# Latent-attention layer: context products in other slots, probabilities turned straight behind the scores, the first group's rows gathered and mixed by tiles

## The reference, cut to what matters

```
x = x + experts(layernorm(x))                       # end of layer 0: slots_out gathered by slot, weighted by wt
h = layernorm(x)
kv = h @ Wkv_down.T ; q = h @ Wq.T ; k = kv @ Wk_up.T ; v = kv @ Wv_up.T
x = x + (softmax(q k^T / 8) v) @ Wo.T               # latent attention
h = layernorm(x)
q = h @ xWq + bq ; k = ctx @ xWk + bk ; v = ctx @ xWv + bv
x = x + softmax(masked(q k^T / 4)) v @ xWo + bo     # cross-attention
x = x + ffn(layernorm(x))                           # quantised gate, up and down products
```

## Time and profile before

| what | value |
|---|---|
| median of three launches | 1798.15 us (1794.9 to 1802.68) |
| the profiled launch | 1803.34 us, its span from first to last instruction 1801.6 us |
| busy share of the span | PE 87%, DVE 53%, ACT 46%, POOL 26% |
| mean granted TensorE clock | 0.931 |
| layer1's slots (first scores to last scores) | 986.5 to 1414 us of the span |

### The profile page before, as it was taken

The page is one execution under the profiler, slowest core; times in us unless marked ns, Lnnn a source line. Parts: engine busy times, 40 slices in busy tenths (PEclk is TensorE's granted clock), DMA queues, the critical chain, the costliest instruction groups (busy, mean ns, idle before and its releaser), DMA issues. The chain is left out here.

```text
span 1801.6 us, 26868 instructions
## 1 busy us (share of the span) xinstructions
PE 1563.5 (87%) x10059; PEld 1083.7 (60%) x10059; DVE 960.3 (53%) x2226; ACT 828.9 (46%) x1819; POOL 459.5 (26%) x582
## 2 busy tenths in 40 slices
PE   6999999998986569999995999999999869994099
PEld 3666766666664348878783666666667634441088
DVE  3555666756765324222213655656564545499932
ACT  3346564554555212121212556556565523596740
POOL 3123223243334310000005654544433200131000
PEclk9999999998988679999996999999999979996599
DMA  3330111111221153353433111110100000000211
GB/s 107 141 145 20 44 28 40 32 41 40 58 80 39 56 165 123 105 158 106 143 108 106 36 37 31 51 51 13 28 16 16 13 12 0 1 0 1 93 35 59
DMA packets 99681, 107.12 MB, mean 59 GB/s; under 512 B 25315, under 2 KB 88557, under 8 KB 99553
## 3 DMA queue, kind: packets, MB, share of 16 engines
q1 hardware_dynamic: 93408, 88.83, 15.7%
q0 software_dynamic: 6144, 16.57, 2.8%
HBM read 63.59 MB, written 42.01 MB: 59 GB/s over the span
## 5 line engine op out<-in xcount | busy, mean ns | idle before, releaser
L1866 ACT ACTIVATE c_pr<-bank,c_nmax 128x256 f32<-128x256 f32 x256 | 117.9, 475 | 153.7 <-DVE c_nmax L1947 131.8
L1619 POOL TENSOR_SCALAR c_pr<-c_pr,c_rsum 128x256 f32<-128x256 f32 x256 | 127.6, 513 | 228.3 <-DVE c_rsum L1952 228.2
L1336 PE MATMUL bank<-b_XT,shared 128*128 128x320 f32 x512 | 154.6, 437 | 0.0
L1386 ACT ACTIVATE b_G<-bank 128x320 f32<-128x320 f32 x128 | 55.9, 437 | 210.9 <-PE bank L1336 210.9
L1350 PE MATMUL bank<-shared,b_G 128*128 128x256 f32 x640 | 142.2, 379 | 0.0
L1350 PEld LDWEIGHTS bank<-shared,b_G 128*128 128x128 f32 x640 | 120.9, 190 | 17.8
L947 DVE TENSOR_TENSOR a_A<-bank,a_causal 128x512 f32<-128x512 f32 x128 | 79.5, 683 | 77.4 <-PE bank L475 77.4
L1947 DVE TENSOR_REDUCE c_nmax<-bank 128x2 f32<-128x512 f32 x128 | 82.3, 684 | 59.0 <-PE bank L1658 58.2
L1336 PEld LDWEIGHTS bank<-b_XT,shared 128*128 128x128 f32 x512 | 92.5, 193 | 27.6 <-issue 1.2
L412 POOL TENSOR_TENSOR a_L<-a_L,a_Lm 128x1232 f32<-128x1232 f32 x32 | 72.0, 2249 | 141.5 <-DVE a_Lm L962 135.9
L1405 DVE COPY b_Y<-bank 128x256 f32<-128x256 f32 x80 | 34.0, 425 | 120.3 <-PE bank L1350 120.1
(11 more groups left out here) (314 smaller groups left out, 3448.7 us busy)
## 6 DMA issues: line engine op xcount, KB each, us to landing
shared<-L_ffn_w SPq DMA_DIRECT2D x32, 512.0 KB
t_slots_in<-a_h SPq DMA_DIRECT2D x20, 512.0 KB, 6.8
shared<-t_slots_in SPq DMA_DIRECT2D x15, 640.0 KB, 7.0
t_slots_out<-b_Y SPq DMA_DIRECT2D x15, 640.0 KB, 4.1
a_xin<-x SPq DMA_DIRECT2D x8, 512.0 KB, 3.8
a_xr<-x SPq DMA_DIRECT2D x8, 512.0 KB, 3.8
t_x_a<-hT_all SPq DMA_DIRECT2D x8, 512.0 KB, 2.9
shared<-t_x_a SPq DMA_DIRECT2D x8, 512.0 KB
```

What stands on the lines that cost most here:

```text
L1336: t = p.matmul(P[2 + n % 2][:, 0:HC], w1[e % 3][:, u, 128 * f:128 * f + 128], XT[e % 2][:, u, HC * m:HC * m + HC], start=(u == 0), stop=(u ...
L1619: p.tensor_scalar(pr[k][:, e, u, :], pr[k][:, e, u, :], rsum[k][:, e, u:u + 1], 1.0, ALU.mult, ALU.mult).then_inc(q.pr_ready, 1)
L1866: a.activation(pr[t % 2][:, e, u, :], P[e][:, S * u:S * u + S], ACT.Exp, bias=nmax[t % 2][:, e, u:u + 1], accum_out=sums[t % 2][:, e, u:u ...
```

## The change

It does the following, all in layer1:

- turn(t - 1) on PE moves to right behind scores(t), ahead of values(t - 2) and all extra work.
- xk and xv are made in slot 7 of their own group, ahead of project0, and copied out by ACT in slot 0 of the next group, behind heads and ahead of the xturn and q3 copies. (Before: made in slot 1, copied in slot 2.)
- xm is made in slot 1, behind turn_norm 0, and copied in slot 2 (before: 3 and 4). penalties runs in slot 2 behind moments(2) (before: slot 4, ahead of by_key).
- vo is made in slot 2 behind project1, and its addition runs in slot 3, ahead of by_key (before: both in slot 5).
- UNITS follows, so that banks 5 to 7 are handed out in another order. By that order the bank of xturn (or of q3 in group 1) is the one that xk held, the bank of q3 is that of xv, turn0b has xout0's, xm has xout1's, latk has lat's and q0 has turn2a's.
- The first group's gathers are issued tile by tile (both choices of tile 0, then of tile 1, and so on), each tile with a semaphore of its own; mix_first waits for one tile at a time, adds both choices and takes that tile's bn_stats.

```diff
--- before.py
+++ after.py
@@ -1499,13 +1499,14 @@
         xPT = sb("xPT", [S2, T])
         amax = sb("amax", [128, 1])
 
-        q = signals(nc, st, "c_pool c_dve rows0 rows1 stored "
+        q = signals(nc, st, "c_pool c_dve tile0 tile1 tile2 tile3 rows0 rows1 stored "
                             "absorb_psum absorb_kept mixed st0 st1 st2 mo0 mo1 mo2 ve0 ve1 ve2 rs0 rs1 rs2 h0 h1 h2 sh0 sh1 sh2 "
                             "s_psum nmax_ready exp_ready rsum_ready pr_ready pt_psum PTa_ready PTd_ready a_psum aT_ready "
                             "kept_dve L_kept L_ready xmax_ready xe_ready xr_ready  amax_part amax_ready "
                             "made0 made1 made2 kept0 kept1 kept2")
         sq = c.second_signals
         r_in, x_in, rows_in = (sq.slot0_in, sq.slot1_in), (sq.x0_in, sq.x1_in), (q.rows0, q.rows1)
+        tile_in = (q.tile0, q.tile1, q.tile2, q.tile3)
         stat_s, mom_s, var_s, rstd_s, h_s = ((q.st0, q.st1, q.st2), (q.mo0, q.mo1, q.mo2), (q.ve0, q.ve1, q.ve2),
                                              (q.rs0, q.rs1, q.rs2), (q.h0, q.h1, q.h2))
         shift_s = (q.sh0, q.sh1, q.sh2)
@@ -1521,13 +1522,13 @@
 
 
         UNITS = {0: (("xturn", -2, 1), ("q3", 0, 1), ("xout0", -2, 2), ("xout1", -2, 2)),
-                 1: (("turn0a", 1, 1), ("turn0b", 1, 1), ("xk", -1, 2), ("xv", -1, 2)),
-                 2: (("project1", -1, 1),),
-                 3: (("lat", 1, 1), ("xm", -1, 2)),
+                 1: (("turn0a", 1, 1), ("turn0b", 1, 1), ("xm", -1, 2)),
+                 2: (("project1", -1, 1), ("vo", -1, 1)),
+                 3: (("lat", 1, 1),),
                  4: (("turn2a", -2, 1), ("turn2b", -2, 1), ("latk", 1, 1), ("q0", 1, 1)),
-                 5: (("vo", -1, 1), ("q1", 1, 1), ("turn1a", -1, 1), ("turn1b", -1, 1)),
+                 5: (("q1", 1, 1), ("turn1a", -1, 1), ("turn1b", -1, 1)),
                  6: (("q2", 1, 1), ("xs", -1, 1)),
-                 7: (("project0", 0, 1),)}
+                 7: (("xk", 0, 2), ("xv", 0, 2), ("project0", 0, 1))}
         place, used, filled = {}, [0, 0, 0], [0, 0, 0]
         turn_of = 0
         for t in range(FIRST, LAST):
@@ -1596,7 +1597,7 @@
                             p.wait_ge(q.mixed, 2 * NT * (i - 1))
                     p.indirect_dma_start(out=rows[k][:, m // NT, m % NT, :], out_offset=None, in_=dr["slots_out"],
                                          in_offset=bass.IndirectOffsetOnAxis(ap=slot[k][:, m:m + 1], axis=0),
-                                         bounds_check=SLOTS - 1, oob_is_err=False).then_inc(rows_in[k], 16)
+                                         bounds_check=SLOTS - 1, oob_is_err=False).then_inc(rows_in[k] if i else tile_in[m % NT], 16)
 
                 def deviation(n, i):
 
@@ -1620,10 +1621,10 @@
                                                 ALU.mult, ALU.mult).then_inc(q.pr_ready, 1)
                     if s in (6, 7) and there(g + 3):
                         for m in range(2):
-                            gather(g + 3, 2 * (s - 6) + m)
+                            gather(g + 3, 2 * (s - 6) + m if g + 3 else NT * m + s - 6)
                     if s in (0, 1) and there(g + 2):
                         for m in range(2):
-                            gather(g + 2, 4 + 2 * s + m)
+                            gather(g + 2, 4 + 2 * s + m if g + 2 else NT * m + 2 + s)
 
             @block.tensor
             def _(p):
@@ -1789,6 +1790,8 @@
                     late, behind, ahead = there(g - 2), there(g - 1), there(g + 1)
                     if there(g):
                         scores(t)
+                    if 0 <= t - 1 < NG * NS:
+                        turn(t - 1)
                     if 0 <= t - 2 < NG * NS:
                         values(t - 2)
                     if s == 0 and late:
@@ -1805,21 +1808,16 @@
                         turn_norm(2, g - 2)
                     if s == 4 and ahead:
                         latent_keys(g + 1)
-                    if s == 5 and behind:
+                    if s == 2 and behind:
                         x_outputs(g - 1)
                     if s == 5 and ahead:
                         queries(g + 1, 1)
                     if s == 6 and ahead:
                         queries(g + 1, 2)
-                    if 0 <= t - 1 < NG * NS:
-                        turn(t - 1)
                     if s == 0 and late:
                         x_values(g - 2, 0)
                         x_values(g - 2, 1)
                     if s == 1 and behind:
-                        context("xk", g - 1, xwk)
-                        context("xv", g - 1, xwv)
-                    if s == 3 and behind:
                         x_keys(g - 1)
                     if s == 4 and ahead:
                         queries(g + 1, 0)
@@ -1828,6 +1826,8 @@
                     if s == 6 and behind:
                         x_scores(g - 1)
                     if s == 7 and there(g):
+                        context("xk", g, xwk)
+                        context("xv", g, xwv)
                         project(g, 0)
 
             @block.scalar
@@ -1899,6 +1899,9 @@
                         exponents(t)
                     if 0 <= t - 2 < NG * NS:
                         heads(t - 2)
+                    if s == 0 and behind:
+                        keep_context("xk", g - 1, kbT, bk)
+                        keep_context("xv", g - 1, vbT, bv)
                     if s == 0 and late:
                         keep_unit("xturn", g - 2, xPT[:, :], bank("xturn", g - 2)[0:S2, :])
                     if s == 0 and there(g):
@@ -1906,12 +1909,9 @@
                     if s == 1 and ahead:
                         keep_norm(0, g + 1, [hT0[:, u, :] for u in range(2)])
                     if s == 2 and behind:
-                        keep_context("xk", g - 1, kbT, bk)
-                        keep_context("xv", g - 1, vbT, bv)
+                        keep_unit("xm", g - 1, xm[:, :, :, :].rearrange("p c b k -> p (c b k)"), bank("xm", g - 1)[:, 0:2 * KX])
                     if s == 3 and ahead:
                         keep_unit("lat", g + 1, latT[(g + 1) % 2][:, :], bank("lat", g + 1)[:, :])
-                    if s == 4 and behind:
-                        keep_unit("xm", g - 1, xm[:, :, :, :].rearrange("p c b k -> p (c b k)"), bank("xm", g - 1)[:, 0:2 * KX])
                     if s == 4 and late:
                         keep_norm(2, g - 2, [c.hT_all[:, u, T * (g - 2):T * (g - 2) + T] for u in range(2)])
                     if s == 5 and ahead:
@@ -1960,16 +1960,30 @@
                 def mix(i, k):
                     if k == 0:
                         v.wait_ge(x_in[i % 2], 32 * (i // 2 + 1))
-                        v.wait_ge(rows_in[i % 2], 16 * TOPK * NT * (i // 2 + 1))
+                        v.wait_ge(rows_in[i % 2], 16 * TOPK * NT * ((i + 1) // 2))
                     for j in range(NT):
                         if k:
                             v.wait_ge(q.mixed, 2 * NT * i + j + 1)
                         v.scalar_tensor_tensor(x3[i % 3][:, j, :], rows[i % 2][:, k, j, :], wt[i % 2][:, NT * k + j:NT * k + j + 1],
                                                x3[i % 3][:, j, :] if k else xin[i % 2][:, j, :], ALU.mult, ALU.add).then_inc(q.mixed, 1)
 
+                def mix_first():
+
+                    v.wait_ge(x_in[0], 32)
+                    for j in range(NT):
+                        v.wait_ge(tile_in[j], 16 * TOPK)
+                        for k in range(TOPK):
+                            if k:
+                                v.wait_ge(q.mixed, 2 * j + 1)
+                            v.scalar_tensor_tensor(x3[0][:, j, :], rows[0][:, k, j, :], wt[0][:, NT * k + j:NT * k + j + 1],
+                                                   x3[0][:, j, :] if k else xin[0][:, j, :], ALU.mult, ALU.add).then_inc(q.mixed, 1)
+                        v.wait_ge(q.mixed, 2 * j + 2)
+                        v.bn_stats(stats[0][:, j, :], x3[0][:, j, :]).then_inc(stat_s[0], 1)
+
                 def moments(n, i, x):
-                    for j in range(NT):
-                        v.bn_stats(stats[n][:, j, :], x[:, j, :]).then_inc(stat_s[n], 1)
+                    if n or i:
+                        for j in range(NT):
+                            v.bn_stats(stats[n][:, j, :], x[:, j, :]).then_inc(stat_s[n], 1)
                     v.wait_ge(stat_s[n], NT * (i + 1))
                     if i:
                         v.wait_ge(h_s[n], NT * i)
@@ -2060,11 +2074,10 @@
                         shifts(2, g - 2)
                     if s == 4 and behind:
                         shifts(1, g - 1)
-                        penalties(g - 1)
                     if s == 5 and there(g + 1):
                         wait_full(v, "latk", g + 1)
                         v.tensor_copy(lat[(g + 1) % 2][:, :, :].rearrange("p j r -> p (j r)"), bank("latk", g + 1)[:, 0:NT * LR]).then_inc(freed("latk", g + 1), 1)
-                    if s == 5 and behind:
```

(9 more changed lines are left out.)

## The result

The changed kernel takes **1807.31 us** (median of 7; 1805.38 to 1809.35) against 1798.22 before (median of 7): ratio 1.0047, 95% interval 1.0035 to 1.0060. It is 0.5% slower; the forecast was 1797.9, no change. The profiled launch has a span of 1805.6 us.

What follows compares the result with a forecast made beforehand. PE was taken as the bound (busy 402.5 of layer1's 427.9 us), so only its waits could be won. The terms summed to -0.2 us, 1803.1 profiled; 5.2 off for the median gave 1797.9 us, range 1784 to 1809.

Steps and rivals of the forecast that it cites:

- start: Group 0's tile-wise start: POOL's power, queued behind group 1's gathers, moves only to 968.0; -1.6 us, bounds 0 and -3.4.
- groups 0 and 1, with the extra product: Early turns wait for POOL, busy with gathers: +1.5 us; one more context product made by the last scores: +2.2.
- group 7: Last group with scores: slot 0 has the new wait and little is won, +1.6 us, bounds 0 and +3.
- end: Behind the last scores: vo addition ahead of moments(1); last x_scores +1.5 us later counted from last turn, bounds -1 and +3.
- The new slots, groups 2 to 6: Steady groups: waits of 4.1 us a group against 4.6 before, -2.4 us over five groups, bounds -9 and +6.
- A slot's fixed part: PE's scores, values and turn in every slot: 2.08 us for the first two plus 0.87 for the turn, 2.96.
- Slot 0: xturn waits for ACT's copy out of xk's bank: new wait of 1.7 to 1.8 us, every group from 1 to 7.
- rival D: Start of group 0: the tile-wise start brings nothing, POOL being the queue in front; 1799.5 us, chance 0.10.
- Clock: PE's granted clock over layer1: 5 us lost now, 2 afterwards, so -3 us; bounds -5 and +15.
- Rival B: PE's two waits per group each halve the clock behind them, twelve at 1.7 us; 1816.3 us, chance 0.10.
- Rival C: Turns wait for POOL in all short slots, about 0.5 us each, +15 us; 1812.9 us, chance 0.07.
- Rival A: The waits forecast at slots 0 and 4 are short, half of each, with no clock loss; 1786.3 us, chance 0.23.

Runs made afterwards that it cites:

- Experiments 6: The changed kernel with ACT's two context copies moved from slot 0 to the end of slot 7 and the turn behind values(t - 2): 1784.54 us, ratio 0.9924 to before.
- 8: The kernel before with only the turn moved, to right behind values(t - 2) (the turn third): 1782.08 us, ratio 0.9907.
- 11: The changed kernel with only the turn moved, to right behind values(t - 2): 1799.46 us, ratio 1.0011 to the kernel before.
- experiment 4: The changed kernel with ACT's two context copies moved from slot 0 to the end of slot 7: 1793.96 us, ratio 0.9978 to the kernel before.
- experiment 2: The kernel before with only turn(t - 1) moved, to right behind scores(t) (the turn ahead): 1792.41 us, ratio 0.9971.
- experiments 1: The kernel before with only the first group's gathers and mix done by tiles: 1795.61 us, ratio 0.9992.
- 9: The kernel before with the turn right behind values(t - 2) and the tile-wise first group, no moved context work: 1778.52 us, ratio 0.9885.
- experiments 5: The kernel before with the turn right behind scores and the tile-wise first group, no moved context work: 1790.81 us, ratio 0.9952.
- 10: The changed kernel with context copies in slot 7, the turn behind values, and the last group's vo addition behind moments(1): 1785.47 us, ratio 0.9924 to before.
- 7: The changed kernel with the first group gathered and mixed as before, without tiles: 1810.06 us, ratio 1.0059 to the kernel before.

## Why the prediction was wrong, point by point

It lay inside its range, but on the wrong side of no change: -0.2 us in the sum, 9.1 measured. In the profiled pair, term by term:

| term of the sum | forecast | measured |
|---|---|---|
| start | -1.6 | -4.1 |
| groups 0 and 1, with the extra product | +1.5 + 2.2 | +5.4 |
| groups 2 to 6, with the clock | -2.4 - 3 | -0.4 |
| group 7 | +1.6 | +1.5 |
| end | +1.5 | +5.1 |
| sum | -0.2 | +7.5 |

**The new slots, groups 2 to 6: the step that failed.** I forecast 56.75 us a group: 52.65 of PE's work by slot and 4.1 of waits. 58.13 were measured, of which the named waits are only 3.0 (1.66, 0.20, 0.20, 0.96); so all the rest is 55.11, 2.46 more than I had. Two terms were mis-sized.

The first is "A slot's fixed part, scores, values and turn, is 2.08 us for the first two and 0.87 for the turn: 2.96". It was read off the old order, where the turn stood between other pieces of work, and carried into the new one, where the three take 3.10. A cost read at one neighbour is no cost at another: 0.14 x 8 = 1.12 us a group, 5.6 over five. Experiments 6, 8 and 11 show what the order by itself is worth, turn ahead against turn third: 9.4, 10.3 and 7.9 us in the whole kernel.

The second was put at nothing without a reason. The "4.6" of the old group holds 0.8 us of short pauses that no wait names (57.24 less 3.80 of waits is 53.44, against 52.65 of work); the "4.1" of the new one holds waits alone. The pauses didn't go: beside the 1.12 us of the fixed part the new group has 1.34 us of them, some 0.4 each in slots 4 and 6. That is 6.7 us over five groups. The two errors together are 12.3 us; shorter waits gave 5.4 of it back, and the clock 2.

Two slips of the sums are small beside this: "group 6 has 0.6 less now" isn't in the -2.4, and the chances as worked out in words come to 0.22 for faster and 0.15 for slower.

**The waits were the right ones, and a quarter too long in the sum.** Slot 0: 1.7 to 1.8 forecast, 1.66 on the row, 1.8 by the slot's length, seven times; experiment 4 shows it as the loss that decides (13 us). Slot 1: 0.4 forecast, 0.2 measured. The turn for POOL in slot 4: 0.2 and 0.20. Queries 0: 1.3 and 0.96. x_scores: 0.45, and at most 0.3. I found the wait that makes the change lose and booked it against old waits of the same size. What I didn't see is that the early turn alone takes these from 3.8 to 1.4 us a group (experiment 2), so that the moved slots had at most 1.4 left to win and brought in 1.66 in slot 0 alone.

**The start.** -1.6 forecast by the place of POOL's power. In the changed kernel:

```profile
959.73 0.48 DVE L1978 SCALAR_TENSOR_TENSOR c_x<-shared,wt 128x256 f32<-128x256 f32 x1 [1.21 <-DMA shared<-t_slots_out,slot]
...
961.72 0.17 DVE L1993 TENSOR_SCALAR c_var_eps<-c_mean_var 128x4 f32<-128x4 f32 x1
...
962.08 1.00 POOL L1598 DMA_INDIRECT c_rows<-t_slots_out,slot  x1 [0.30 <-issue]
963.10 1.06 POOL L1605 TENSOR_TENSOR c_rstd<-c_var_eps,c_minus 128x4 f32<-128x4 f32 x1
...
964.75 2.26 PE L1693 MATMUL bank<-ident,c_h 128*128 128x128 f32 x8 [11.34 <-issue]
```

The variance is ready at 961.89 and the power starts at 963.10, right behind the gather, as forecast. From layer1's first matmul (946.79) to the transposes it is 17.96 us instead of 20.02: 2.06 gained (the 1.6, 0.3 by which that gather is now shorter, and 0.1 by which it comes sooner). The Trainium skill (GPSIMD Engine Reference, Key points) names contention between POOL and VectorE instructions with two SBUF inputs; I had weighed that against the tiles. No gather between 948 and 963 pays here, all take 0.99 to 1.06, so the contention didn't come where the additions are two at a time. The profiles of the changed kernel and of experiments 1, 4, 6, 9 and 11 gain another 2 us, as the clock rises earlier in the queries that follow (twelve matmuls in 5.42 us in the changed kernel, 7.21 before); in experiments 5 and 10 it didn't (7.64 us in 5), and the stretch was 33.6 us. Without the tiles it is 35.0 to 35.5 in all five profiles. In medians the tiles are worth 2.8 (7), 1.6 (2 to 5) and 3.6 us (8 to 9), with 95% intervals that overlap each time. By the trace, rival D is out.

**Early turns, groups 0 and 1.** +1.5 and the extra product's 2.2 forecast, +5.4 measured. The early turn alone costs 3.0 (experiment 2), the product 2.1. Group 1's own new wait, 1.6 on queries 3's row and by the length of the group (53.60 us, 51.95 in experiment 4), is in no term of the sum, though I had written "in every group from 1 to 7"; the moved slots win 1.4 back in group 1. The early turns' cost is there in the rows, POOL's product and two gathers between one product and the next:

```profile
986.92 1.85 POOL L1620 TENSOR_SCALAR c_pr<-c_pr,c_rsum 128x256 f32<-128x256 f32 x4
...
988.93 1.09 POOL L1598 DMA_INDIRECT shared<-t_slots_out,slot  x1 [0.16 <-issue]
990.33 1.00 POOL L1598 DMA_INDIRECT shared<-t_slots_out,slot  x1 [0.30 <-issue]
991.37 1.85 POOL L1620 TENSOR_SCALAR c_pr<-c_pr,c_rsum 128x256 f32<-128x256 f32 x4
992.36 0.66 PE L1670 MATMUL bank<-ident,c_pr 128*128 128x128 f32 x4 [0.80 <-POOL c_pr L1620]
```

**Group 7 and the end.** +1.6 forecast for group 7, +1.5 measured. The end: +1.5 forecast, +5.1 measured. turn1's last transposes and x_scores run at half clock in the changed kernel and didn't before; first the kernel before, then the changed one:

```profile
1440.52 1.04 PE L1692 MATMUL bank<-ident,c_h 128*128 128x128 f32 x8
1442.34 1.98 PE L1765 MATMUL bank<-c_xm,c_hT 128*128 128x77 f32 x16 [0.79 <-ACT c_hT L1848]
```

```profile
1440.20 2.72 PE L1693 MATMUL bank<-ident,c_h 128*128 128x128 f32 x8 [2.70 <-ACT c_h L1888]
1443.65 3.67 PE L1766 MATMUL bank<-c_xm,c_hT 128*128 128x77 f32 x16 [0.73 <-issue]
```

Counted from the last scores (1412.78 and 1410.65) the transposes start 1.8 us later; the two pieces then take 1.7 us longer each, 3.4 of the 5.1. (My +1.5 was for x_scores counted from the last turn, which now comes earlier; by that count it is 4.3.) No term of the sum holds the half clock at the end. With less work left for PE behind the last scores, it stands idle ahead of them for 2.70 us; before, x_outputs (3.53 us) lay there. That the idle time halved the clock was argued only.

**Clock.** -3 forecast; the steady groups show no halving at all, so about -5 in the profiled pair. Rival B, twelve halvings, is out: none followed the waits of 1.66 us. Rival C is out in the steady groups, where the turn waits 0.20 us once a group, and true in group 0. Rival A was wrong (the slot 0 wait was no shorter), but experiment 4 shows what it was worth to be rid of it.

## What to carry to other kernels

When a unit's place in one engine's order changes, go through its buffer's next user and ask when, in the releasing engine's own order, the copy comes: here the product was made a slot earlier, its copy stood behind a whole softmax, and the next user came first. When PE is the bound, read the cost of a short product at its new neighbours, not at the old ones. Compare like with like: if the old time holds pauses that no wait names, so will the new one. And take a change apart before judging it: of three parts, the turn was worth -5 us (-16 one place further on), the tiles -2 to -4, and the moved slots +16 with the turn ahead, +21 with it third (9 to 11) and +30 in its old place.

## What the runs showed of the hardware that I had not expected

- The order of three short products that are all there in both cases (scores, values, turn) changes their time: 3.10 us with the 128-row transposes between the two others, 3.01 with them last, and the full product behind them is up to 0.11 us longer in the first case. Weight loads start with their product, at most 0.03 us ahead, at every border with a 64-row or 64-column product in groups 2 to 6 of seven profiles. The shapes were not changed by themselves.
- PE's granted clock stayed at 1.00 behind waits of 1.66 us in all of groups 2 to 6; it was halved behind two of five waits of 2.1 us (before: slots of 10.0 and 10.1 us against 8.4) and behind three of five of 2.67 us. The length of the last wait doesn't decide alone: before, group 2 kept its clock behind 2.12 us in slot 4 and had it halved in slot 7 (8.20 us against 6.56), behind 1.21 us in slot 6, which group 3 had as well without a loss.
- The moment at which the clock rises ahead of the first scores differs between launches of nearly the same code by about 2 us (5.42 and 7.64 us for the same twelve matmuls; early in six and late in two of the eight profiles with the tiles).
